# Two-layer graph network on one core: all of x asked for first, the first adjacency rows held until eight row pairs of x are in

## What is computed

```python
deg = max((adj != 0).sum(-1), 1)
h = max(layernorm(x), 0)
attn_a = sigmoid(concat([adj @ h, h]) @ Wa.T + ba);  attn_b = the same with Wb, bb
g = h @ W_sa;  scores = (g @ a_l)[:, None] + (g @ a_r)[None, :]
e = where(adj != 0, exp(-leaky_relu(scores, 0.01)), 0)
x_a = (e / (e.sum(1) + 1e-5)) @ g
x_b = adj @ (h @ W_gcnb) + b_gcnb
x = x + sigmoid(attn_a * x_a + attn_b * x_b)
h = max(layernorm(x), 0)
x = x + relu(((adj + I) / deg @ h + h) @ W + b)      # dinv * a_hat * dinv, dinv = deg ** -0.5
```

## Time and profile before

| | us |
|---|---|
| median of 3 runs | 672.12 |
| lowest, highest | 670.83, 672.31 |
| profiled execution, span | 671.5 |
| PE busy | 625.2 (93%) |
| DVE busy | 470.2 (70%) |
| ACT busy | 327.2 (49%) |
| POOL busy | 89.8 (13%) |

### The profile page before, as it was taken

One profiled execution on the slowest core, in us unless ns is written; L12 is line 12 of the kernel. 1 busy time (PEld: TensorE's weight loads), 2 busy tenths in 40 slices (PEclk: granted clock), 3 DMA queues, 4 the chain that ended last, 5 costly groups with the idle time before them and its releaser, 6 DMA issues.

```text
span 671.5 us, 15005 instructions
## 1 busy us (share of the span) xinstructions
PE 625.2 (93%) x5488; PEld 544.5 (81%) x5488; DVE 470.2 (70%) x1147; ACT 327.2 (49%) x748; POOL 89.8 (13%) x146
## 2 busy tenths in 40 slices
PE   2289999969999999999999999999989999999994
PEld 1168888858888888888888888888878888888883
DVE  4498889998888989898989899998153234223332
ACT  2168696858576758495857667585020000000000
POOL 4122110202020201102020205010010001000100
PEclk9979999989999999999999999999999999999997
DMA  6945034808080716263544526221134545554441
GB/s 151 230 131 77 1 115 91 204 1 204 0 203 38 165 76 127 102 101 111 92 129 74 149 54 157 46 102 51 51 100 115 155 149 156 147 158 136 147 132 31
DMA packets 28462, 74.85 MB, mean 111 GB/s; under 512 B 3870, under 2 KB 18458, under 8 KB 26777
## 3 DMA queue, kind: packets, MB, share of 16 engines
q1 hardware_dynamic: 11202, 48.24, 21.6%
q0 software_dynamic: 14272, 22.14, 19.5%
q10 hardware_dynamic: 2967, 4.20, 2.7%
HBM read 71.15 MB, written 25.56 MB: 144 GB/s over the span
## 4 chain that ended last, share of the span: by engine, by line
PE 67%; issue 9%; DVE 7%; ACT 1%; POOL 1%; ACTq 0%; DVEq 0%; POOLq 0%
PE accA L576 10%; PE accA L577 10%; PE accA L570 8%; PE accA L571 8%; PE accE L586 8%; PE accE L588 8%; PE accE L587 8%; DVE Z L854 3%; DVE E L861 2%; PE dA L595 1%; PE dA L597 1%; PE dA L596 1%; PE tp L562 1%; PE dB L595 1%; PE dB L597 1%
## 5 line engine op out<-in xcount | busy, mean ns | idle before, releaser
L586 PE MATMUL accE<-h,Z 128*128 128x257 f16 x676 | 185.7, 275 | 0.4 <-DVE E L861 0.4
L588 PE MATMUL accE<-h,E 128*128 128x257 f16 x676 | 184.9, 273 | 0.0
L587 PE MATMUL accE<-h,Z 128*128 128x256 f16 x676 | 184.3, 273 | 0.0
L854 DVE SCALAR_TENSOR_TENSOR Z<-adjT,vr,Z 128x256 f32<-128x256 bf16 x338 | 147.8, 481 | 21.0 <-ACT Z L413 18.8
L570 PE MATMUL accA<-adjT,h 128*128 128x256 bf16 x676 | 157.4, 277 | 0.0
L571 PE MATMUL accA<-adjT,h 128*128 128x256 bf16 x676 | 157.3, 277 | 0.0
L576 PE MATMUL accA<-h,adjT 128*128 128x257 f16 x676 | 149.8, 273 | 1.9 <-DVE wm L1086 1.1
L408 ACT ACTIVATE Z<-slp,sr 128x256 f32<-128x256 f32 x338 | 150.3, 496 | 2.4 <-PE accE L588 1.1
L577 PE MATMUL accA<-h,adjT 128*128 128x256 f16 x676 | 149.8, 273 | 0.0
L861 DVE TENSOR_TENSOR E<-Z 128x512 bf16<-128x512 f32 x169 | 115.0, 686 | 0.5
L413 ACT ACTIVATE Z<-Z 128x512 f32<-128x512 f32 x169 | 102.9, 617 | 0.0
(11 more groups left out here) (114 smaller groups left out, 628.4 us busy)
## 6 DMA issues: line engine op xcount, KB each, us to landing
adjT_store<-adjT SPq DMA_DIRECT2D x13, 1664.0 KB, 5.4
stage<-in_adj_dram POOLq DMA_DIRECT2D x36, 416.0 KB, 6.9
adjT<-adjT_store SPq DMA_DIRECT2D x26, 512.0 KB, 4.6
adjT<-adjT_store SPq DMA_DIRECT2D x13, 640.0 KB, 3.9
stage<-in_adj_dram POOLq DMA_DIRECT2D x12, 415.5 KB, 9.7
out_dram<-osb ACTq DMA_DIRECT2D x12, 256.0 KB
xs<-in_x_dram SPq DMA_DIRECT2D x5, 256.0 KB, 11.6
xs<-in_x_dram SPq DMA_DIRECT2D x3, 320.0 KB
```

The source lines that it names most:

```text
L586: pe.matmul(accE[e][:, 0:D + 1], zhi, h1[0][:, t, 0:D + 1], start=(t == 0), stop=False)
L587: pe.matmul(accE[e][:, 0:D], zhi, h2[0][:, t, :], start=False, stop=False)
L588: ins = pe.matmul(accE[e][:, 0:D + 1], zlo, h1[0][:, t, 0:D + 1], start=False, stop=(t == TILES - 1))
L854: ins = dve.scalar_tensor_tensor(out=Z[:, u, v], in0=rows, scalar=vr[:, t:t + 1], in1=Z[:, u, v], op0=ALU.mult, op1=ALU.mult)
```

## The change

Two edits. SP issues x groups 2 and 3 right behind group 1; the four bias loads and the wait for `w_in` come after them. POOL waits for the four DMAs of x group 2 (with groups 0 and 1, eight row pairs) ahead of adjacency pair 0.

```diff
             for g in range(1, len(GROUPS)):
                 load_x(sp, g)
-                if g == 1:
-                    for e in range(2):
-                        for k, w in enumerate((ba, bb)):
-                            src = bass.AP(w.tensor, 0, [[0, P], [1, 1]])
-                            sp.dma_start(bias4[:, e, 1 + k:2 + k], src).then_inc(bias_in, 16)
-                    sp.wait_ge(w_in, 16 * N_WDMA)
+            for e in range(2):
+                for k, w in enumerate((ba, bb)):
+                    src = bass.AP(w.tensor, 0, [[0, P], [1, 1]])
+                    sp.dma_start(bias4[:, e, 1 + k:2 + k], src).then_inc(bias_in, 16)
+            sp.wait_ge(w_in, 16 * N_WDMA)
...
             pool.wait_ge(pads, 1)
+            pool.wait_ge(x_in[2], 16 * 4)
             load_adj(0)
```

## The result

| | before | changed |
|---|---|---|
| median of 7 runs, us | 672.31 | 676.59 |
| lowest, highest | 670.83, 674.50 | 675.00, 679.58 |
| profiled execution, span | 671.5 | 677.0 |

The ratio is 1.0058, with a 95% interval of 1.0037 to 1.0079: slower by 0.6%, 3.9 us of 672. The forecast was no change, 672.0 us, and the range ended at 674.2.

What follows compares the result with a forecast made beforehand. Start-up bound by x and adjacency reaching DVE's turning, then PE: 27.6 - 3.3 + 2.3 + 0.7 + 0.3 = 27.6 against 27.72, -0.1 us; span 671.4, plus 0.6 for the runs' median, 672.0 us; range 669.4 to 674.2.

Steps and rivals of the forecast that it cites:

- What bounds the start-up: DVE's turning of adjacency pair 0 at 27.72 us starts its full stretch; x and adjacency both arrive just in time.
- That a shift passes through to the end: From the turning on every engine keeps its order, so the -0.1 us reaches 42.9 us and the end unchanged.
- rival D: PE's half clock from 42.9 to 52.9 us may move: at most 2.7 us faster (0.05) or 2 us slower (0.04).
- The gap filled: The DMA engines' nearly empty 3.3 us, from 8.9 to 12.2, can be filled with x group 2.
- POOL's start: POOL, waiting for x group 2, goes on at about 14.5 us instead of 8.36, including 1.2 us for the landing.
- the sum: Adjacency landing: 27.6 - 3.3 for the gap + 2.3 for x ahead + 0.7 + 0.3 losses = 27.6 us.
- POOL's whole delay free: x group 3 keeps the engines busy from 13.3 to 18.9 us, so adjacency latency up to 4.4 us costs nothing.
- The view by conserved bytes: Of x, 0.54 MB formerly behind the last adjacency byte now comes ahead of it, costing 2.3 us.
- the biases and the later weights: On SP's queue behind x: biases done by 27.5 us, later weights landed by 35, before DVE reads them; free.
- a ragged end: Adjacency load ending alone has slow last slices: 0.3 us added to its landing.
- The bounds: Adjacency landing between 25.1 us (-2.6) and 29.8 us (+2.1, latency 5.2 us and nothing overlapping).
- rival B: POOL's queue delivers first adjacency bytes late, mattering from 4.4 us latency; at 5.2 us +2.1 us, 674.2 us; chance 0.13.

Runs made afterwards that it cites:

- e1: Changed kernel without POOL's wait for x group 2, so SP's reordering alone: turning at 29.69 us, ratio to the kernel before 1.0028.
- e2: Kernel before with only POOL's wait for x group 2 added, SP's order unchanged: turning at 35.39 us, ratio to before 1.0102.
- e3: Changed kernel with SP's later weights held until adjacency pair 0 has landed: turning at 32.22 us, ratio to before 1.0056.
- e4: Changed kernel with the 31-row load of x split into 16 and 15 rows: turning at 34.19 us, ratio to before 1.0091.
- e5: Changed kernel with the 31-row load split and the later weights held until adjacency pair 0 has landed: turning at 29.23 us, ratio to before 1.0023.
- e12: Changed kernel without POOL's wait, 31-row load split, later weights held until adjacency pair 0 has landed: turning at 27.07 us, ratio to before 0.9981.
- e6b: Against the kernel before: biases behind x group 2, x group 3 only once adjacency pair 0 has landed, no POOL wait: turning at 25.70 us, ratio 1.0015.
- e8: Kernel before with the four bias loads moved behind x group 3, SP's wait for first weights left in place: turning at 25.19 us, ratio 1.0005.
- e9: Kernel before with the four bias loads moved between x groups 2 and 3: turning at 24.21 us, ratio 1.0013.

## Why the prediction was wrong

**What bounds the start-up: right.** In every experiment where the turning waited for the adjacency and nothing behind it was late (e1 to e5, e12) DVE read the later weights 10.35 us behind it, before 10.54, and the ratio followed: 27.07 gave 0.9981, 29.23 gave 1.0023, 29.69 gave 1.0028, 32.22 gave 1.0056, 32.58 gave 1.0058, 34.19 gave 1.0091, 35.39 gave 1.0102. In e6b, where x group 3 was late behind it, it was 14.8 us.

**That a shift passes through to the end: right, with a little on top in the trace.** 4.9 us at the turning are 5.5 us of span. The rest came between 122 and 160 us: POOL's `ve` ahead of three adjacency pairs in a row begins at 121.57, 153.00 and 186.43 before and at 126.47, 158.66 and 191.84 in the changed kernel, 4.9, 5.7 and 5.4 us later. From 140 to 160 us the granted clock is 0.91 before and 0.83 in the changed kernel, and PE's instructions in the stretch are 130 and 111; what lowered it further is open:

```profile
140.00:160.00 20.00, 15.94 (x130) 13.54 (x131) 17.13 (x35) 11.71 (x28) 4.15 (x7) 0.91 0.43 120
```

```profile
140.00:160.00 20.00, 14.62 (x111) 11.67 (x110) 17.54 (x40) 11.87 (x28) 1.18 (x3) 0.83 0.16 65
```

The half-clock stretch in PE's full part (rival D) is there in both, 42.9 to 52.9 before (granted 0.51) and 47.6 to 57.8 now (0.50). Over all runs the change costs 3.9 us, so the profiled execution is one of the longer ones.

**The gap filled: right.** 227 GB/s from 9 to 12 us.

**POOL's start: too early by 1.9 us.** The forecast was 14.5 for x group 2; the issues came at 16.35. The bytes came as the sum had it, 2.60 MB from 2 to 13 us, but the landing was 3.3 us behind them. I had put 1.2 us there, with no row for it. I called POOL's whole delay free, as long as group 3 keeps the engines busy. It is not: e12 to e5 says 2.16 us, most of it by the lower rate of what then runs without x.

**When the adjacency lands: the step that failed.** The sum gave 27.6, it was 32.6. The view by conserved bytes named what must come ahead of the last adjacency byte as x alone. Behind x in SP's queue stand the biases and the later weights, and I took these to begin only at 30.5, since 258 bias packets had taken 3 us in the gap. That was a bad row for their rate: in the microsecond ahead of it, 8 to 9 us, SP's queue had moved 232. In the changed kernel the 4-byte packets went much faster too, 913 packets of under 512 B in the 2 us behind 18:

```profile
DMA packets 1076, 0.30 MB, mean 152 GB/s; under 512 B 913, under 2 KB 1002, under 8 KB 1076
```

So the weights came beside the adjacency, 0.67 MB of them, 2.8 us at 0.235. Before they had been behind it, and POOL's early issue was what kept them there: by moving POOL's issue from 8.4 to 16.4 the change moved it past them. And the sum treated the 16 engines as one: beyond 0.3 us for a ragged end it had no term for one engine that is behind with its share of the adjacency. Before, SP's loads had such a tail too (a DMA share of 0.08 from 33.5 to 34 us), but nobody waited there; in the changed order the adjacency stands behind x, and so behind this engine's share of it. These two terms measured 3.35 us together.

**The bounds.** The upper one, 29.8, took the software queue's delay at its longest row, 5.2 us; e1 and e4 show 6 and 5.1. In the changed kernel itself the delay was about 2.4 us (issue at 16.35, three packets before 18.5, 16 in the next half microsecond, 34 in the one behind it), well under the 4.4 from which rival B decides. So B's mechanism was not what happened, though its sign, a turning above 29.1, was there. The bound left out the same terms as the sum. With what they measured, 3.35 us for weights and engine and 2.16 for POOL's wait, the sum of 27.6 becomes 33.1, against the 32.6 in the trace.

## What to carry to other kernels

When a load is made to wait, list everything that will be queued ahead of it by then, on every queue, and not only what it was meant to wait for: an early issue also keeps later loads out. In a start-up bound by loads look at the ends of the DMA rows as well as at their middle; a tail with a share near one sixteenth may be one engine, and a load whose rows don't divide among the engines may be what put it behind. Two causes, one behind the other, hide each other: neither the hold nor the split gained anything to speak of alone, together they gave back 3.35 us.

## What the runs showed of the hardware

A queue whose first issue meets another, full one is not served evenly from the start. Of POOL's queue behind SP's nothing moved for 6 us in e1 while SP's queue moved 613 packets between 9 and 14 us, and 1 packet against 1563 moved from 18 to 22 us in e4; in e2, issued at 18.48, its first packets came at 23; with SP's queue empty (e8) it took 1.5 us. It holds the other way round too: in e8 SP issued x group 2 at 9.6 us with its own queue empty, when POOL's had just started, and the first bytes came at 13.2; in e9 it was 9.1 and 12.4. Once both ran, they shared nearly evenly. The Trainium skill, "DMA: Bandwidth & Descriptors", section "Queues, rings and completion order", has each engine change between queues after a packet of typically 9 to 17 and at most 64 descriptors. If a packet that the profile counts is one such descriptor, which no run here shows, 613 over 16 engines are 38 each, which that would allow, and 1563 are 98 each, more than one such turn. What decides when the second queue comes in stays open here.

A single issue can hold the issuing engine for microseconds while its queue has much to move: SP stood in two of them for 3.4 and 3.6 us in the changed kernel, and for 1.7 and 0.9 us in the same two in e4, where one load of 62 KB had been split. That a full queue is what holds it was not shown.

The loads of one 4-byte element for each partition moved 258 packets in 3 us when they were alone (before, 9 to 12 us), but 232 in the one microsecond ahead of it, beside ACT's loads, and 913 in 2 us in the changed kernel, where the weights' 4-byte loads were among them. Why they were slow in the first case was not tried.
